# First expert layer: blocks in another order, the first 17 from three chunks' counts, and no gathers of blocks

## The reference, cut to what matters

```
x = x + ffn0(cond0(x))                 # dense, 1024 wide
x = x + moe1(cond1(x))                 # 32 experts, the 4 best per token, 96 wide
x = x + ffn2(attention2(x))            # paged attention, few tokens
x = x + moe3(cond3(x))                 # 8 experts, the 2 best per token, and a shared one

# moe1, for a token t:
w, e = top_k(softmax(t @ gate), 4);  w = w / w.sum()
out = sum_j w_j * ((u * silu(g)) @ down[e_j]),  (g, u) = split(t @ gate_up[e_j])
```

## Time and profile before

| | us |
|---|---|
| median of 3 runs | 994.47 (993.54 to 2144.03) |
| the profiled execution | 991.54 |
| its span, first to last instruction | 989.7 |
| PE / DVE / POOL / ACT busy | 836.8 / 572.1 / 391.5 / 349.0 |

### The profile page before, as it was taken

The page is one execution under the profiler, slowest core; times in us unless marked ns, Lnnn a source line. Parts: engine busy times, 40 slices in busy tenths (PEclk is TensorE's granted clock), DMA queues, the critical chain, the costliest instruction groups (busy, mean ns, idle before and its releaser), DMA issues.

```text
span 989.7 us, 16462 instructions
## 1 busy us (share of the span) xinstructions
PE 836.8 (85%) x5237; PEld 677.0 (68%) x5237; DVE 572.1 (58%) x1679; ACT 349.0 (35%) x1007; POOL 391.5 (40%) x411
## 2 busy tenths in 40 slices
PE   1999998950899997677479897979997989999997
PEld 1787776730789996666357676869555757777786
DVE  5546888562478866296368787762363443444243
ACT  3334352421333332112257686712253222222211
POOL 7300528175666767484355443000067002334000
PEclk9999998985899999789589899997998989999999
DMA  8235103769565652672476776200433102332222
GB/s 341 64 117 139 61 27 103 272 189 276 165 206 164 175 166 65 222 263 82 103 155 161 159 157 137 101 1 1 138 103 119 60 6 83 102 99 73 86 73 98
DMA packets 67239, 126.42 MB, mean 128 GB/s; under 512 B 20004, under 2 KB 49085, under 8 KB 64515
## 3 DMA queue, kind: packets, MB, share of 16 engines
q1 hardware_dynamic: 45407, 74.42, 24.8%
...
...
## 4 chain that ended last, share of the span: by engine, by line
PE 34%; DMA 9%; DVE 2%; SPq 2%; ACT 2%; issue 1%; DVEq 0%; POOLq 0%; ACTq 0%
PE ps L462 9%; PE ps L739 5%; PE ps L773 3%; DMA early<-newblk,new_i 3%; DMA big<-early 3%; DMA early<-early 2%; SPq L1015 2%; DMA early<-in_cache,win_i 2%; PE ps L2417 2%; PE ps L2314 1%; PE ps L2462 1%; PE ps L2356 1%; PE ps L2283 1%; PE ps L2418 1%; PE ps L2305 1%
## 5 line engine op out<-in xcount | busy, mean ns | idle before, releaser
L845 POOL DMA_INDIRECT sent_d<-mid,slot_i x88 | 97.8, 1112 | 111.9 <-DVE mid L623 66.3
L786 ACT ACTIVATE early<-ps 128x256 f32<-128x256 f32 x134 | 51.3, 383 | 182.4 <-PE ps L752 182.4
L836 POOL DMA_INDIRECT back_d<-early,mid x95 | 94.5, 995 | 44.6 <-issue 34.3
L804 DVE TENSOR_TENSOR early<-early,ps 128x96 f32<-128x96 f32 (+1 forms) x134 | 37.3, 278 | 108.5 <-ACT early L792 95.6
L773 PE MATMUL ps<-early 96*128 (+1 forms) x346 | 97.1, 381 | 0.2
L496 DVE TENSOR_TENSOR hidl<-work,hidh 128x512 fp32r<-128x512 f32 (+1 forms) x56 | 38.7, 692 | 84.7 <-ACT hidh L489 84.7
L502 ACT ACTIVATE work<-ps 128x512 f32<-128x512 f32 (+1 forms) x56 | 33.3, 595 | 140.5 <-PE ps L462 140.3
L836 POOL DMA_INDIRECT back_d<-big,mid x39 | 38.4, 984 | 111.9 <-DVE big L818 109.6
L739 PE MATMUL ps<-big,early 128*128 x380 | 79.0, 330 | 0.2 <-issue 0.2
L752 PE MATMUL ps<-late,mid 128*128 128x128 f32 x268 | 52.7, 279 | 27.7 <-DMA mid<-sent_d,first_i 26.2
L739 PEld LDWEIGHTS ps<-big,early 128*128 128x128 f32 x380 | 67.6, 192 | 5.8 <-issue 0.8
...
## 6 DMA issues: line engine op xcount, KB each, us to landing
...
```

Source lines behind the costliest of these rows:

```text
L786: nc.scalar.activation(L.yTb[b % ring_y], ps[:, b % 2, 0:2 * P], ACT.Copy).then_inc(s["turn_sb"], 1)
L804: nc.vector.tensor_tensor(L.hb[j % ring_h], L.sgb[j % 2], ps[:, 2 + j % 2, F:2 * F], ALU.mult)\
L836: nc.gpsimd.indirect_dma_start(out=back_d, out_offset=bass.IndirectOffsetOnAxis(ap=xblk[b % XRING][:, D:D + 1].bitcast(I32), axis=0), in_= ...
L845: nc.gpsimd.indirect_dma_start(out=sent_d, out_offset=bass.IndirectOffsetOnAxis(ap=L.slot_i[:, i:i + 1], axis=0), in_=L.rows[c][:, t, n, : ...
```

## The change

The order of the first expert layer's blocks is new. When three chunks are counted, `dve_early` makes a table (`early_i`) of the first 17 blocks (`EARLY`): every expert has given at most 127 rows to a block that is not full, so 3 x 512 x 4 pairs hold at least 17 full blocks. These go to buffers of their own (`xearly`, in `yT` and `low0`), and DVE writes their results over them. Behind them come the other full blocks by the final counts, then the partly filled ones, by the table that `dve_rest` makes in eight parts between DVE's first block steps; PE turns it at block 8 (`TABLE_AT`). At least 33 blocks are full (`SURE`), so the fills must be there from block 33 on. All 32 fills are issued by SP, eight per seven blocks from block 2 on (`fills_before`). POOL's ten gathers and `dve_firsts` are gone, and so is the old table of `dve_ends` for this layer. PE starts the blocks when chunks 0 to 2 are sent, while POOL still sends chunk 3. ACT's copies of chunk 3's last two tiles stand behind its blocks 0 and 1; their PSUM banks are 6 and 7 instead of 0 and 1. The next layer's weights are loaded behind block 41 instead of 16, and the mask steps begin at 14 instead of 4.

```diff
-AT_FILLS, AT_COLS, AT_TABLE, AT_FIRSTS = range(1, 5)
-GOT_FIRST = (("castb", 80),) + (("seggot", 48),) + (("sent30", 32),) * 2 + (("sent31", 48),) * 3 + (("sent32", 48),) * 3
-FIRSTS = len(GOT_FIRST)
-FIRST3 = (32, 48, 48)
+AT_FILLS, AT_COLS, AT_TABLE = range(1, 4)
+TABLE_AT = 8
+EARLY = ((NCH - 1) * CH * K1 - E1 * (P - 1) + P - 1) // P
+SURE = (PAIRS - E1 * (P - 1) + P - 1) // P
...
-L1.gathered, L3.gathered = FIRSTS, 0
+L1.early, L3.early = EARLY, 0
...
+        yflat = yT[:, :, :].rearrange("p k t -> p (k t)")
+        inyT = KD * T // ROWW
+        xearly = [yflat[:, j * ROWW:(j + 1) * ROWW] for j in range(min(EARLY, inyT))]
+        xearly += [low0[:, j * ROWW:(j + 1) * ROWW] for j in range(EARLY - inyT)]
...
-        ROW_BANKS = [[5, 4, 5, 4]] * (NCH - 1) + [[5, 4, 0, 1]]
+        ROW_BANKS = [[5, 4, 5, 4]] * (NCH - 1) + [[5, 4, 6, 7]]
...
-            if t == 2 and c == NCH - 1:
-                pe.wait_ge(s["hfull_ready"], NCH * M0)
...
-        def dve_firsts(dve, ch, L):
...
+        def dve_early(dve, ch):
+
+            L, E = L1, E1
+            dve.wait_ge(s["slots_ready"], NCH - 1)
...
+            ch.link(nc.vector.tensor_tensor(counts, L.running, C["region"][:, 0:E], ALU.subtract))
+            ch.link(nc.vector.tensor_scalar(floors, counts, 1.0 / P, 0.5 / P - 0.5, ALU.mult, ALU.add))
+            ch.link(nc.vector.tensor_scalar(counts, floors, MAGIC, None, ALU.add))
+            ch.link(nc.vector.tensor_scalar(floors, counts, MAGIC, None, ALU.subtract))
+            ch.link(nc.vector.tensor_tensor_scan(until, C["ones"][:, 0:E], floors, 0.0, ALU.mult, ALU.add))
+            ch.link(nc.vector.tensor_scalar(past, until, C["blockno"], None, ALU.is_le))
+            ch.link(nc.vector.tensor_reduce(owner, past, X, ALU.add))
+            ch.link(nc.vector.tensor_tensor(counts, past, floors, ALU.mult))
+            ch.link(nc.vector.tensor_reduce(spent, counts, X, ALU.add))
+            ch.link(nc.vector.tensor_tensor(row, C["blockno"], spent, ALU.subtract))
+            ch.link(nc.vector.tensor_scalar(spent, owner, float(SPAN1), None, ALU.mult))
+            ch.link(nc.vector.scalar_tensor_tensor(row, row, float(P), spent, ALU.mult, ALU.add))
+            ch.link(nc.vector.tensor_scalar(cols2[:, 0:1], row, float(E * SPAN1), None, ALU.min))
+            nc.vector.tensor_scalar(cols2[:, 1:2], owner, float(E - 1), None, ALU.min).then_inc(s["tables"], 1)
+            ch.link(nc.vector.tensor_scalar(counts, until, -1.0, float(EARLY), ALU.mult, ALU.add))
+            ch.link(nc.vector.tensor_tensor(counts, counts, floors, ALU.add))
+            ch.link(nc.vector.scalar_tensor_tensor(L.taken, counts, 0.0, floors, ALU.max, ALU.min))
...
+        def dve_rest(ch, part):
...
+            if part == 0:
+                nc.vector.memset(L.bases[:, 2 * E:2 * E + 1], float(SPARE1))
+                ch.link(nc.vector.tensor_tensor(counts, L.running, C["region"][:, 0:E], ALU.subtract))
+                ch.link(nc.vector.tensor_scalar(rounded_up, counts, 1.0 / P, 0.5 / P - 0.5, ALU.mult, ALU.add))
+                ch.link(nc.vector.tensor_scalar(L.floors, rounded_up, MAGIC, None, ALU.add))
+            elif part == 1:
+                ch.link(nc.vector.tensor_scalar(L.floors, L.floors, MAGIC, None, ALU.subtract))
+                ch.link(nc.vector.tensor_tensor(full, L.floors, L.taken, ALU.subtract))
+                ch.link(nc.vector.scalar_tensor_tensor(partial, L.floors, float(P), counts, ALU.mult, ALU.is_lt))
...
+                nc.vector.tensor_tensor(cols2[:, 1:2], owner, wrap, ALU.add).then_inc(s["tables"], 1)
+
+        def dve_early_table(dve):
+            dve.wait_ge(s["table_ps"], 1)
+            nc.vector.tensor_copy(L1.early_i[0:2, :], ps[0:2, 3, 256:276]).then_inc(s["tables"], 1)
+
+        def pe_early_table(pe):
+            pe.wait_ge(s["tables"], 1)
+            nc.tensor.matmul(ps[0:2, 3, 256:256 + P], L1.tabf[:, 36:38], ident, start=True, stop=True)\
+                .then_inc(s["table_ps"], 1)
...
                                                             skip_runtime_bounds_check_because="the table holds values within these bounds")[1]
+
+        def numbers(L, row, b, engine, most):
+            if b < L.early:
+                g = b - b % 4
+                return zip(range(g, g + 4), four_values(L.early_i[row:row + 1, g:g + 4], engine, most))
+            g = b - L.early - (b - L.early) % 4
+            return zip(range(L.early + g, L.early + g + 4), four_values(L.table_i[row:row + 1, g:g + 4], engine, most))
+
+        def rows_in(L, b):
+            return xearly[b] if b < L.early else xblk[(b - L.early) % XRING]
+
+        def rows_out(L, b):
+            return xearly[b][:, 0:D] if b < L.early else L.ob[b % ORING]
...
         def sp_block(sp, L, b, starts):
 
-            if b >= L.gathered + AHEAD:
+            if b >= AHEAD:
                 sp.wait_ge(s["turn_ps"], L.turn0 + b - AHEAD + 1)
-            if b >= XRING:
+            if b >= L.early + XRING:
                 j = (b - XRING) % ORING
                 sp.wait_ge(s["gone%d" % j], L.gone0[j] + 16 * ((b - XRING) // ORING + 1))
-            if b not in starts:
-                g = b - b % 4
-                starts.update(enumerate(four_values(L.table_i[0:1, g:g + 4], mybir.EngineType.SP, SPARE1), g))
-            sp.dma_start(xblk[b % XRING], sent_d[bass.ds(starts[b], P), :]).then_inc(s["into%d" % (b % AHEAD)], 16)
+            if b == L.early or (b if b < L.early else b - L.early) % 4 == 0:
+                starts.update(numbers(L, 0, b, mybir.EngineType.SP, SPARE1))
+            sp.dma_start(rows_in(L, b), sent_d[bass.ds(starts[b], P), :]).then_inc(s["into%d" % (b % AHEAD)], 16)
...
-        FILLS = [[e for e in range(E1) if e % 2 == 0 or e >= 28], list(range(1, 28, 2))]
+        def fills_before(b):
+            return min(E1, max(0, (b - 2) * 8 // 7))
...
-            sp.wait_ge(s["tables"], AT_FILLS)
-            for e in FILLS[0]:
-                r = sp.value_load(L1.endrow_i[0:1, e:e + 1], min_val=e * SPAN1, max_val=e * SPAN1 + T)
-                sp.dma_start(*fill_rows(r, e)).then_inc(s["filled"], 16)
-            sp.wait_ge(s["tables"], AT_TABLE)
-            sp.wait_ge(s["filled"], 16 * E1)
-            sp.wait_ge(s["cond"], 32)
+            sp.wait_ge(s["tables"], 2)
             for name in ("sent", "sent_late"):
-                sp.wait_ge(s[name], NCH * HALF_SENT)
+                sp.wait_ge(s[name], (NCH - 1) * HALF_SENT)
             starts = {}
-            for b in range(FIRSTS, NBK):
+            for b in range(NBK):
+                if b == EARLY:
+                    sp.wait_ge(s["tables"], L1.table0 + AT_TABLE)
+                    for name in ("sent", "sent_late"):
+                        sp.wait_ge(s[name], NCH * HALF_SENT)
+                if b == SURE:
+                    sp.wait_ge(s["filled"], 16 * E1)
+                    sp.wait_ge(s["cond"], 32)
                 sp_block(sp, L1, b, starts)
-                if b == XRING:
+                if b == 2:
+                    sp.wait_ge(s["tables"], L1.table0 + AT_FILLS)
+                    sp.wait_ge(s["fill_set"], 2)
+                for e in range(fills_before(b), fills_before(b + 1)):
+                    r = sp.value_load(L1.endrow_i[0:1, e:e + 1], min_val=e * SPAN1, max_val=e * SPAN1 + T)
+                    sp.dma_start(*fill_rows(r, e)).then_inc(s["filled"], 16)
+                if b == EARLY + XRING + 2 * ORING:
                     sp.dma_start(mid[:, 4160:5696], a["l2w"][:, 0:1536]).then_inc(s["wqkv"], 16)
                     sp.dma_start(raw3, a["raw3"]).then_inc(s["raw3"], 16)
...
-            pool.wait_ge(s["tables"], AT_FIRSTS)
-            pool.wait_ge(s["cond"], 32)
-            for name in ("sent", "sent_late"):
-                pool.wait_ge(s[name], NCH * HALF_SENT)
-            for b in range(FIRSTS):
-                gather(xblk[b].bitcast(I32), sent_d.bitcast(I32), L1.first_i[:, b:b + 1], s[GOT_FIRST[b][0]])
             for b in range(NBK):
                 pool_block(pool, L1, b)
...
-            act.wait_ge(s["tables"], AT_FILLS)
-            act.wait_ge(s["fill_set"], 2)
-            for n, e in enumerate(FILLS[1]):
-                if n == 2:
-                    act_copies(act, NCH - 1, 2)
-                    act_copies(act, NCH - 1, 3)
-                    nc.scalar.activation(warm[:, 1:2], C["ones"][:, 0:1], ACT.Silu)
-                r = act.value_load(L1.endrow_i[0:1, e:e + 1], min_val=e * SPAN1, max_val=e * SPAN1 + T)
-                act.dma_start(*fill_rows(r, e)).then_inc(s["filled"], 16)
-
+            nc.scalar.activation(warm[:, 1:2], C["ones"][:, 0:1], ACT.Silu)
             for b in range(NBK + L1.lag):
                 act_block(act, L1, b)
+                if b in (0, 1):
+                    act_copies(act, NCH - 1, 2 + b)
 
             act.wait_ge(s["index"], AT_FOLDS)
...
+                    if tc == NCH - 1 and m == 7:
+                        dve_early(dve, ch)
...
             dve_adapter(dve, NCH - 1)
```

(32 more changed lines are left out.)

109 lines of the change are left out of this document (59 added, 50 removed).

## The result

On the chip the changed kernel takes 995.71 us (median of 20 runs, 987.44 to 1009.03) and the kernel before, beside it, 989.35: a ratio of 1.0059, 95% interval 1.0033 to 1.0084. On another chip later the two gave 997.52 and 988.32, 1.0088 (1.0058 to 1.0119). So the change costs 6 to 9 us where I had forecast a gain of 4. The time lay in my range and within 2%; the sign was wrong. The miss in the time alone, 5.2 us against 990.5, flatters the forecast: it was counted from the 994.47 of three runs, and from the 989.35 of 20 runs it would have been 985.4, a miss of 10.

What follows compares the result with a forecast made beforehand. PE waited for block 0 until 249.32; afterwards SP's queue would bound 27 blocks. Block 0 16.8 us earlier leaves 5.5 at block 30, less 1.55: net 4.0, so 991.54 becomes 987.5 (median 990.5), range 976 to 1003.

Steps and rivals of the forecast that it cites:

- Part 1: Start of the expert blocks: PE's block 0 begins at 232.5 instead of 249.32, 16.8 us earlier.
- DVE's chain: On DVE ahead of the last chunk's residual: 17 early-table operations and a copy push later work back 2.3 us.
- Part 2: SP between blocks 3 and 30: fills at 1.25 us make SP's turn 2.04 against PE's 1.413; block 30 only 5.5 us earlier.
- The stop for the large loads: PE's wait behind two large weight loads moves from block 16 to 41, past block 30, so 1.55 us is lost again.
- Sum: Whole kernel: block 30 comes 5.5 us earlier, 1.55 is lost again at the large loads, net 4.0 us gained.
- SP does not bind: Rival, blocks from 5 on: a fill costs below 0.7 us, PE keeps 1.413; gain 16.8 us, 977.7; chance 0.17.
- Slower fills under load: Rival, SP between blocks 3 and 30: fills cost 1.64 us (time 1002, chance 0.13) or 2.1 (1016, 0.05); loss from 1.38.
- The change does not move the start: Rival, block 0: its load and the sends delay each other, start 238 to 240; 6 to 8 us less gain, 997; chance 0.10.
- Part 3: The rest (POOL's gathers, chunk 3's last sends, scatters, DVE's tables, other waits): hidden or released early, counted at nothing.
- The Trainium skill's four-at-a-time rule: SP's fills: register loads have a 600 ns floor, so unroll four; by it a fill costs 0.93 us, 9.6 us better.

Runs made afterwards that it cites:

- zmdown: fills4 with the six down-weight loads (3.1 MB) moved behind block 3's load and the mask rows' load behind block 8's; 4 us slower than fills4.
- later: The changed kernel with the early table's DVE operations and PE matmul moved out of the last chunk's chain; 995.11 us against 995.71.
- pieces_again: The changed kernel with only the two large loads behind block 41 cut into six pieces, one every four blocks; 996.13 us against 997.52 on the same chip.
- fills4: The changed kernel with the row numbers of SP's 32 fills read four at a time, 8 loads instead of 32; 985.8 us against 995.7.
- pieces4: fills4 with the two large loads behind block 41 cut into six pieces, one every four blocks; 980.7 us against 985.8.
- dup_bytes: fills4 with each fill sent a second time, to rows nobody reads (4.3 MB more); 41 us slower than fills4 by the medians.
- zl_fill1: pieces4 with the mask rows' load behind block 8's and each fill in 128 packets of 1040 bytes; 971.39 us, 0.9835 of the kernel before.

## Why the prediction was wrong, step by step

- **Part 1, block 0 at 232.5 (16.8 us earlier): right in size.** From the end of the dense layer 29.4 us were forecast; the two profiles show 28.4 and 30.6 (gains of 17.8 and 15.6). The reason, the queue of weights ahead, is what zmdown showed. DVE's chain, which I charged at 2.3 us, did not delay SP's issue of block 0 (`later`: 21.4 us behind the dense layer without it, 20.8 and 21.6 with it), so that the size came out is in part luck.
- **Part 2, the fill at 1.25 us and SP's turn at 2.04: right in kind, too small; this is the step that failed.** SP did become the bound. But block 0 to block 30 took 61.5 and 64.8 us where the forecast had 56.4 (232.5 to 288.9), 5.1 and 8.4 more. SP's own stretch, the issue of block 4 to that of block 30, was forecast at 53.4 us and took 56.2 and 59.8: the blocks cost what I had said (0.62 and 0.64 against 0.61), the fills 1.34 and 1.43 us instead of 1.25, around the 1.38 from which my "slower" rival decides. Between block 0's transposes and block 4's issue lay 1.6 us in both profiles, not 0.7, and the landing of block 30 took 3.65 and 3.4 instead of 2.3. The rows show in part why a fill cost more than in those from which I took its price, 242.1 to 249.6. The DMA instruction ahead of it is now mostly that of a block, 0.37 and 0.41 us on average in the two profiles against the 0.32 of a fill's, and the register load took 0.46 and 0.52 us on average against 0.45. It was not that I had taken rows with emptier engines: they were 0.79 busy there and 0.81 in the new stretch. Why single register loads take anything from 0.27 to 1.13 us is open. Six steps of a row that varies so much were too few for a term that is counted 30 times, where 0.13 us more turn the gain into a loss.
- **The stop for the large loads, "1.55 lost again": too small.** Blocks 30 to 94 took 95.2 and 93.7 against 92.0 forecast. In the first profile that was 2.99 us at block 42 instead of 1.55, and 1.4 us for block 31 at the lower clock; in the second the stop was the 1.55 of the forecast, and the 1.4 us of block 31 came on top. pieces_again bounds what the loads cost in the time at about 1 to 2 us, within its uncertainty.
- **Sum:** 4.0 forecast; by the marks of ACT, +1.0, -5.1, -3.2 make a loss of 3.3 in the first profile, -1.2, -8.4, -1.7 one of 7.3 in the second. The medians say 6.4 and 9.2 lost; the 2 to 3 us between come from outside the stage, or from executions unlike the profiled one, and were not traced.
- **Rivals.** "SP does not bind" was wrong for this kernel, and fills4 and pieces4 show what it would have given: not 16.8 us against the kernel before, but 1.6 (not clear of the noise), and 7.2 with the stop at block 42 gone as well. That the DMA engines, at 0.86, stand behind SP is argued from dup_bytes and zl_fill1 and not shown by itself: in fills4 SP still issued its blocks up to 3.2 us later than PE allowed. "Slower fills under load" was the nearest in price; its 0.13 was too little. "The change does not move the start" was wrong.
- **Part 3 at nothing** held in kind: chunk 3's last send began at 240.36, and POOL and DVE ended in time. What I had not costed is the granted clock behind PE's waits for the early table and the residual; `later` shows it in the trace and nothing in the time.
- **The Trainium skill's four-at-a-time rule** I had used for an estimate of 9.6 us better than my sum. The load itself was cheaper than the Trainium skill's floor (0.35 us in the median), but the fill cost 1.34 and 1.43 us and not 0.93, since some 0.5 us of check and register operations stand beside the load and the DMA instruction. What the rule says to do, four numbers at a time, was right here: 10 to 14 us.

Why the change as such lost: it moved 32 fills, 4.3 MB and 20 or more microseconds of SP and ACT, out from beside the sends, where PE had nothing to do, to between the block loads. Blocks 0 to 30 became 16.7 to 20.0 us longer, 0.5 to 0.6 a fill, which is the whole of what the earlier start gave; 12.2 to 15.5 of them go with the single register loads (fills4: 49.3), the other 4.5 stay. With the loads in fours, the pieces, the small packets and the mask rows' load behind block 8, the same order of blocks is 1.65% faster than the kernel before (interval 1.2 to 2.1%). How much of that the kernel before would gain from the small packets too was not measured.
